# A perceiver block: waits of a step's four mask matmuls, one by one instead of all together

## The reference

```python
energy = jnp.einsum('bhqd,bhkd->bhqk', Q, K) * scale
energy = jnp.where(m == 0, -1e9, energy)
attn = jax.nn.softmax(energy, axis=-1)
out = jnp.einsum('bhqk,bhkd->bhqd', attn, V)
```

## Time and profile before

| what | us |
|---|---|
| median of 3 runs | 776.03 |
| lowest and highest run | 775.78, 777.36 |
| span of the profiled execution, first to last instruction | 779.7 |
| its 48 looped steps from 136.27 on | 298.11 |
| TensorE busy | 682.9 (88%) |
| DVE busy | 621.1 (80%) |
| ACT busy | 470.1 (60%) |

### The profile page before, as it was taken

How to read it: one execution, slowest core, us unless ns; L and a number is a source line. 1 busy time by engine, 2 the same in 40 slices (tenths; PEclk the granted TensorE clock), 3 DMA queues, 4 the chain that set the end, 5 groups by cost and what they waited for, 6 DMA issues and landing times.

```text
span 779.7 us, 29152 instructions
## 1 busy us (share of the span) xinstructions
PE 682.9 (88%) x9915; PEld 534.1 (68%) x9915; DVE 621.1 (80%) x1462; ACT 470.1 (60%) x1499; POOL 417.4 (54%) x439
## 2 busy tenths in 40 slices
PE   4732999999999999999999975599999949999995
PEld 2421767777777777777777754478777737888894
DVE  6413899999999999999999966769888956779584
ACT  2731767777777777777777743435555533545552
POOL 4650385465455456354453417757777747506376
PEclk9985999999999999999999998979999957999998
DMA  7497444444444444444443003000000020002531
GB/s 169 98 160 183 84 95 87 89 87 96 88 89 96 84 92 95 85 97 85 83 81 67 1 3 108 2 3 4 4 0 0 4 68 2 1 1 83 192 116 42
DMA packets 186526, 55.05 MB, mean 71 GB/s; under 512 B 146708, under 2 KB 184856, under 8 KB 186466
## 3 DMA queue, kind: packets, MB, share of 16 engines
q1 hardware_dynamic: 183344, 49.88, 30.4%
q0 software_dynamic: 1824, 3.96, 1.5%
q10 hardware_dynamic: 1298, 0.40, 0.2%
HBM read 44.51 MB, written 8.83 MB: 68 GB/s over the span
## 4 chain that ended last, share of the span: by engine, by line
PE 59%; SPq 14%; issue 8%; ACT 6%; DVE 6%; POOL 4%; ACTq 1%; DMA 1%; DVEq 0%; POOLq 0%
PE bank L484 25%; PE energy L484 20%; PE bank L487 14%; SPq L515 9%; ACT PR L632 5%; DVE STAT L1531 2%; SPq L521 2%; SPq L538 1%; POOL SX L923 1%; POOL TQ L915 1%; DMA MK<-in_mask_BxSxS_ik 1%; PE energy L487 1%; ACTq L632 1%; SPq L503 1%; SPq L506 0%
## 5 line engine op out<-in xcount | busy, mean ns | idle before, releaser
L632 ACT ACTIVATE PR<-energy,STAT 128x256 f32<-128x256 f32 x512 | 234.8, 484 | 116.8 <-DVE STAT L1531 116.8
L1531 DVE TENSOR_REDUCE STAT<-energy 128x512 f32 (+1 forms) x256 | 164.3, 685 | 27.1 <-PE energy L484 26.9
L487 PE MATMUL bank<-ident,PR 128*128 128x128 f32 x1024 | 151.9, 282 | 31.6 <-DVE PT L1548 28.0
L1548 DVE COPY PT<-bank 128x512 f32<-128x512 f32 x256 | 161.8, 671 | 0.8 <-PE bank L487 0.8
L487 PEld LDWEIGHTS bank<-ident,PR 128*128 128x128 f32 x1024 | 109.3, 141 | 62.6 <-issue 50.9
L820 POOL TENSOR_TENSOR QB<-QT,headmask 128x512 f32<-128x512 f32 x32 | 33.3, 1041 | 191.2 <-DMA MK<-in_mask_BxSxS_ik 121.9
L632 ACT ACTIVATION_READ_ACCUMULATOR PR<-energy,STAT (+1 forms) x512 | 110.4, 216 | 0.0
L827 POOL TENSOR_SCALAR MZ<-MK 128x512 bf16<-128x512 int32 x64 | 94.3, 1490 | 7.2 <-DMA MK<-in_mask_BxSxS_ik 7.2
L484 PEld LDWEIGHTS bank<-wv_s,CT 128*128 128x128 f32 x512 | 67.2, 192 | 31.3 <-issue 31.3
L1504 DVE STREAM_TRANSPOSE CT<-CX 128x512 f32<-128x512 f32 x64 | 44.9, 701 | 32.3 <-DMA CX<-in_ctx 29.3
L484 PE MATMUL bank<-PT,VT 128*32 128x128 f32 x2048 | 70.0, 278 | 0.3 <-DVE PT L1548 0.3
(11 more groups left out here) (265 smaller groups left out, 1295.6 us busy)
## 6 DMA issues: line engine op xcount, KB each, us to landing
CX<-in_ctx SPq DMA_DIRECT2D x512, 32.0 KB, 2.5
MK<-in_mask_BxSxS_ik SPq DMA_DIRECT2D x128, 128.0 KB
rows_in<-fill SPq DMA_DIRECT2D x1, 3483.0 KB, 21.2
X<-in_x SPq DMA_DIRECT2D x4, 512.0 KB, 7.3
VLT<-v_last SPq DMA_DIRECT2D x4, 512.0 KB, 9.8
PAY<-rows_in SPq DMA_DIRECT2D x2, 903.0 KB, 8.2
PAY<-X SPq DMA_DIRECT2D x1, 1280.0 KB, 6.8
w_s<-in_L_ffn_W SPq DMA_DIRECT2D x1, 1024.0 KB, 5.6
```

The costliest lines, as they stand in the source:

```text
L487: return nc.tensor.transpose(o, i, ident[0:n, 0:n])
L632: nc.scalar.activation(PR[:, b, g, :], EB[:, g, e * KEYS:(e + 1) * KEYS], ACT.Exp, bias=STAT[:, bass.ds(t, 1), b, 1, g:g + 1].rearrange("p ...
L1531: V.tensor_reduce(STAT[:, bass.ds(t, 1), b:b + 2, 1, g:g + 1].rearrange("p a b g -> p (a b g)"), EB[:, g, :].rearrange("p (e k) -> p e k", ...
L1548: V.tensor_copy(PT[:, k % 2, e, 2 * half:2 * half + 2, :].rearrange("p g k -> p (g k)"), psum[1 if e else 7]).then_inc(ev_t, 1)
```

## The change

The one wait for all eight exponents of the step before, ahead of the four mask matmuls, is replaced by one wait ahead of each: bank g waits for 8p - 6 + 2g, which is the count when both exponents of that bank have been made (for g = 3 this is 8p). In step 0 nothing is waited for, as before.

```diff
             def energies(i, r):
                 p, k, t = pair(i, r)
                 pe.wait_ge(pool_m, p + 1)
-                wait_reuse(pe, act_exp, 8 * p)
                 for g in range(NG):
+                    if not (isinstance(p, int) and p == 0):
+                        pe.wait_ge(act_exp, 8 * p - 6 + 2 * g)
                     rows = slice(32 * g, 32 * g + 32)
                     mm(EB[:, g, :], SEL_Q[rows, :], MZ[rows, k, :, :].rearrange("p e k -> p (e k)"), stop=False)
                 pe.wait_ge(ev_k, p + 1)
```

## The result

| | before | after |
|---|---|---|
| median of 20 runs, us | 776.06 | 778.90 |
| ratio of the runs | | 1.0032, 95% interval 1.0018 to 1.0046 |
| span of the profiled execution, us | 779.7 | 776.9 |
| instructions in it | 29152 | 29256 |

What follows compares the result with a forecast made beforehand. TensorE was busiest (88%), and bank 3's series was taken to end each attention step. Head cost 13 x 0.21 = +2.8 us, less 0.26, gave +2.5: 776.03 to 778.5 us, range 775.4 to 781.2.

Steps and rivals of the forecast that it cites:

- What the last mask sets: Attention steps on PE: bank 3's series of mask and four passes ends the step; starting banks 0 to 2 earlier gains nothing.
- The ceiling of 0.085 a turn: Mask starts in the loop: most any gain could be, all masks at PE's own 0.205 us; 1.1 us over 13 turns.
- The number of instructions: PE's sequencer, looped steps: 8p-4 and 8p-2 are new register instructions, 2 x 0.105 us; 8p at bank 3 taken as free.
- The head: First step of each turn, behind the branch: added register work is uncovered and delays bank 3's mask, 0.21 us a turn.
- The cover elsewhere: Second to fourth steps: transposes and the exponent wait hide the register work within 0.46 us, 0.1 to spare.
- The gain of second and fourth steps: Bank 3's load leaves first on the release rather than fourth: some 0.01 us per place, 0.26 us in all.
- B: Rival at PE's waits: bank 3's value is computed too, waits cost 51 ns apiece, or both; 779.9 to 781.9 us, chance 0.20.
- C: Rival at the turn's head: a late head is made up for in later steps; within 1 us of 776.0, chance 0.20.
- D: Rival at the mask matmuls: the banks' early masks count, so the kernel is faster; 774.9 us, chance 0.10.
- E: Rival on PE's sequencer: each wait value takes two chained instructions; +18.5 us, 794.5, chance 0.02.
- "ACT PR": Sign in the lines view: the eighth exponent as what ended the mask loads' idle, 9.2 us before, would be nearly gone.
- 50 to 100 ns of the Trainium skill: Semaphore reads at 13 heads: three more waits each would add an estimated 2.0 to 3.9 us, 780.5 to 782.4.

Runs made afterwards that it cites:

- two waits: Kernel before, with banks 0 to 2 sharing a wait for 8p-2 and bank 3 waiting for 8p; 44 steps 272.61 us against 272.94, ratio 0.9993.
- loop cut elsewhere: PE's loop turns behind energies instead of ahead of it; with the change's four waits, 44 steps 271.92 us against 272.94 before, ratio 0.9997.
- three waits: The change without bank 0's wait; 44 steps 274.01 us against 272.94 in the kernel before, ratio 1.0041.

## Why the prediction came out right

- **What the last mask sets: right.** It was the reason to expect no gain, and the run with bank 3's mask alone bears it out. Early masks by themselves are worth 0.03 a turn (two waits) or 0.04 (four, loop cut elsewhere), with a scatter of 0.02. The ceiling of 0.085 a turn stood for all first masks at PE's own 0.205; that is what the two kernels with the loop cut elsewhere and two or four waits do, and they are 0.09 to 0.10 ahead.
- **The number of instructions: right.** Two more in a looped step, 8p free.
- **The head: right to 0.01.** Forecast 0.21 a turn and a step of 6.42; the step shown takes 6.42. In the mean of eleven heads bank 3's load comes 0.38 behind the exponent instead of 0.17. The parts are off and cancel: the loads spread by 0.23 more than before, not 0.21, and the first of them comes 0.02 sooner behind the exponent, not 0.014 later.
- **The cover elsewhere: right, and too careful.** Four instructions hide in the middle steps too. The "0.1 to spare even with a third" doesn't follow from the 0.46 it stands beside (0.46 - 0.31 - 0.105 leaves 0.04); up to the load itself, at 421.94, it does.
- **The gain of second and fourth steps: right.** Forecast 0.01 each; bank 3's load comes 0.052 behind the exponent instead of 0.061. A turn lost 0.17, not 0.19; the remaining 0.02 is no more than two traces differ by. 13 x 0.17 = 2.2 us, against a forecast of 2.5 and a measured 2.5 (1.4 to 3.6): the total can't tell the two apart. That forecast and total agree to the tenth is luck, since with three waits the total was 2 us off what the steps explain.
- **The rivals.** B, a third instruction or 51 ns a wait: neither is there; constant waits cost nothing. C, a head that makes up for its delay: it doesn't, since doubling the added instructions doubled the loss. D, the ceiling: reached with the loop cut elsewhere, not by the change. E: one instruction per value.
- **What was wrong** is one sign to look for. "ACT PR" was to be all but gone from the mask loads' idle in the lines view; it is still 8.3 us of 9.1. I had shown that this idle is mostly PE's own pause, and should have seen that its label would stay. And the 50 to 100 ns of the Trainium skill for reading a semaphore from the sequencer (Advanced Engine Details and Errata, Network/Comms) don't appear at all for a wait that rides on a weight load and is already met: three more in each step left the 44 steps at 272.82 against 272.94.

## What to carry to other kernels

A wait for a computed value isn't free: on PE's queue each register instruction took 0.1 us, and it counts where the sequencer has nothing queued ahead, above all behind a loop's branch. Before a wait is split, ask which part ends the work, since the other parts win nothing, and count what the split puts on the queue; then cut the loop where the engine has a microsecond of work in flight (0.05 us a turn here, too little for a total to show), or write it out (0.8% here), and look at the queues of the other engines too. Idle time that a view puts down to a semaphore is a gain only if the work could have started without it, so compare starts, not idle sums.

## What the runs showed of the hardware

- A register instruction on PE's queue lasts 32 to 50 ns but takes about 0.1 us of its time where nothing covers it: turns 0.10, 0.17 and 0.35 longer with one, two and four more at the head. Under transposes it cost nothing.
- Waits for values long reached cost nothing when they ride on a weight load: 3 x 64 more left the loop as it was, 272.82 against 272.94. An EVENT_SEMAPHORE of its own behind the last semaphore cost 0.07 (417.84 to 417.96, against 0.05 before).
- Steps with computed values take 6.16 to 6.22 us and undisturbed steps with constants 6.05, at the same granted clock of 1.00 and with the same matmuls. In the step shown the minima start 0.11 sooner behind the masks and the first exponent 0.13 sooner behind the minima. That the register work of DVE and ACT is the reason is argued from this; the kernels differ in their branches and in the length of their code as well.
- On PE 0.205 us pass between the start of the last transpose and that of the first mask, in every step where nothing else holds the mask; between two transposes it is 0.11.
